# Feed-forward, attention, feed-forward of a macaron layer: three phases one after the other, or one phase in which the feed-forwards run piecewise inside the attention of a neighbouring batch

## The reference

```python
x = x + 0.5 * ffn(layernorm(x))                 # first feed-forward, gives x1
x = x + attn(layernorm(x))                      # gives x2
x = x + 0.5 * ffn(layernorm(x))                 # last feed-forward, same weights

def fp4(x):      # blocks of 16 along the last axis
    scale = max(max|block| / 6, 1e-12)
    return round |block| / scale to {0, .5, 1, 1.5, 2, 3, 4, 6}, sign back, * scale

def ffn(x):      # 128 -> 352 -> 128, every operand through fp4
    h = silu(fp4(x) @ fp4(w_gate).T) * (fp4(x) @ fp4(w_up).T)
    return fp4(h) @ fp4(w_down).T

def attn(x):     # 16 heads of 64, softmax over 512 keys
    o = softmax(q @ k.T / 8) @ v
    y = o @ w_proj + b_proj + x
    return layernorm(y, eps=1e-6) * gamma + beta
```

## Time and profile before

| | us |
|---|---|
| median of 3 runs (2581.35 to 2583.0) | 2582.26 |
| profiled execution, its own time | 2578.82 |
| span from the first to the last instruction | 2577.0 |
| mean granted clock of PE | 0.931 of 2.4 GHz |
| busy: PE, DVE, ACT, POOL | 2293.6, 1475.1, 1248.3, 1320.6 |

### The profile page before, as it was taken

The page is one execution under the profiler, slowest core; times in us unless marked ns, Lnnn a source line. Parts: engine busy times, 40 slices in busy tenths (PEclk is TensorE's granted clock), DMA queues, the critical chain, the costliest instruction groups (busy, mean ns, idle before and its releaser), DMA issues. The chain is left out here.

```text
span 2577.0 us, 39199 instructions
## 1 busy us (share of the span) xinstructions
PE 2293.6 (89%) x13353; PEld 1218.7 (47%) x13353; DVE 1475.1 (57%) x2161; ACT 1248.3 (48%) x1848; POOL 1320.6 (51%) x852
## 2 busy tenths in 40 slices
PE   3768759999999999999999999999999999566776
PEld 2545524545444444444444444444445455244444
DVE  5898844455445444544444444445445455389986
ACT  3555535455545445544544454455445455344454
POOL 3565625555545555555554555555555555355553
PEclk8887769999999999999999999999999999677778
DMA  4100000000000000000000000000000000000100
GB/s 122 33 25 25 19 21 6 2 6 7 2 7 2 6 3 6 6 2 7 2 6 3 6 2 6 7 2 6 2 7 2 6 2 2 18 17 26 31 20 21
DMA packets 182697, 32.50 MB, mean 13 GB/s; under 512 B 149184, under 2 KB 176000, under 8 KB 182528
## 3 DMA queue, kind: packets, MB, share of 16 engines
q1 hardware_dynamic: 182528, 30.17, 6.5%
HBM read 15.42 MB, written 8.39 MB: 9 GB/s over the span
## 5 line engine op out<-in xcount | busy, mean ns | idle before, releaser
L852 DVE TENSOR_REDUCE nmax<-pX 128x2 fp32r<-128x1024 f32 x512 | 626.9, 1225 | 336.6 <-PE pX L912 323.3
L795 POOL TENSOR_TENSOR ES<-ES,E 128x1024 f32<-128x1024 f32 x256 | 607.9, 2375 | 337.6 <-ACT E L807 337.5
L807 ACT ACTIVATE E<-pS 128x1024 f32<-128x1024 f32 x512 | 524.5, 1024 | 467.0 <-PE pS L901 392.6
L791 POOL TENSOR_TENSOR ES<-E 128x1024 f32<-128x1024 f32 x128 | 303.8, 2373 | 555.7 <-ACT E L807 555.7
L927 PE MATMUL pO<-E,VA 128*64 128x512 f32 x2048 | 555.5, 621 | 0.0
L885 PE MATMUL pM<-xf,w_raw 128*64 128x512 f32 x1024 | 268.6, 603 | 8.5 <-DMA xf<-xhT 6.2
L901 PE MATMUL pS<-QH,KH 64*128 64x512 f32 x1024 | 256.0, 497 | 19.4 <-issue 19.3
L901 PEld LDWEIGHTS pS<-QH,KH 64*128 64x128 f32 x1024 | 95.5, 183 | 358.6 <-ACT E L807 183.8
L865 DVE TENSOR_TENSOR ON<-OT,pM 128x512 f32<-128x512 f32 x128 | 88.0, 687 | 263.7 <-PE pM L971 263.7
L912 PE MATMUL pX<-KH,QH 64*128 64x512 f32 x1024 | 231.6, 416 | 4.0 <-DVE nmax L852 2.6
L901 PE MATMUL pS<-SH,onesr 64*128 64x512 f32 x1024 | 203.5, 394 | 0.0
(11 more groups left out here) (145 smaller groups left out, 3167.0 us busy)
## 6 DMA issues: line engine op xcount, KB each, us to landing
RROW<-RC SPq DMA_DIRECT2D x512, 2.0 KB, 2.0
Fxin<-in_L_attn_x SPq DMA_DIRECT2D x16, 256.0 KB, 2.7
Y<-in_L_attn_x SPq DMA_DIRECT2D x16, 256.0 KB, 4.8
x<-Fxout SPq DMA_DIRECT2D x16, 256.0 KB, 2.0
xf<-xhT SPq DMA_DIRECT2D x16, 256.0 KB, 2.3
SH<-nmax SPq DMA_DIRECT2D x256, 2.0 KB, 2.0
LC<-LROW SPq DMA_DIRECT2D x256, 2.0 KB, 2.0
Lx1in<-x SPq DMA_DIRECT2D x16, 256.0 KB, 2.7
```

Source lines behind the costliest of these rows:

```text
L791: g.tensor_tensor(ES[par][:, :, :], E[0][:, :, :], E[1][:, :, :], ALU.add).then_inc(s_add, 1)
L795: g.tensor_tensor(ES[par][:, :, :], ES[par][:, :, :], E[s][:, :, :], ALU.add).then_inc(s_add, 1)
L807: a.activation(E[s][:, :, :], pS[:, :, :], ACT.Exp).then_inc(s_exp, 1)
L852: v.tensor_reduce(nmax[px % 2][:, :, t:t + 1], pX[:, :, :], AX.X, ALU.max, negate=True).then_inc(s_max, 1)
```

## The change

One program without phases. In the 32 steps of attention of batch b run pieces of the first feed-forward of batch b + 1 and of the last one of batches b - 1 and b - 2. A table by step number t = 4 p + s says which piece; each engine has four such functions (`first_ffn_psum`, `last_ffn_psum` before the step's own work, `first_ffn`, `last_ffn` behind it; on PE and POOL only the last two). Steps run over b from -2 to 17, so that batch -1 has only the first feed-forward of batch 0 and batches 16 and 17 have only the ends.

- Each feed-forward has one PSUM bank, `pF`, through which turned x, gate tiles, up tiles, turned h tiles and the down product go one after the other. Silu of g is made as g (1 + tanh(g/2)) / 2: tanh on ACT, two operations on DVE.
- h is quantized in two halves (704 elements per partition each) and in place.
- All feed-forward matmuls, the turns too, are ordinary products in halves of 64 output rows.
- The projection of a pair goes into `pX[:, 0]` and DVE adds it to `Yacc` in SBUF; `pY` and the matmul that loaded it from `Y` are gone. On PE the projection now stands ahead of K.
- x1, the norm of x1 and y stay in SBUF for two batches; the DRAM tensor, `xhT` and `Y` are gone. x is loaded and the result stored by SP once a batch, in the fifth and the fourth pair.
- POOL's sums over the exponential are two operations of 512 each instead of one of 1024.
- V's tiles run three rounds ahead instead of four.

What runs at which step t (b is the batch of the attention around it; F is the first feed-forward, L the last):

| engine | F of b + 1 (norm and rounding of x: b + 2) | L of b - 2 (t to 11), of b - 1 (from t = 10) |
|---|---|---|
| PE | turn x 0, gate 1-4, up 5-8, turn h 12-15, down 16, turn x1 20 | up 0-2, turn h 6-9, down 10; turn x 26, gate 27-30, up 31 |
| ACT ahead of the exponential | copy x 1, tanh 2-5, copy h 13-16, copy x1 21 | copy h 7-10; copy x 27, tanh 28-31 |
| ACT behind | magic h 9, 11; scale x1 19; scale x 22; magic x 25 | magic h 3, 5; scale y 13; scale x2 18; magic x 22 |
| DVE ahead of the maxima | silu 2-5, h 6-9, x1 = pF + xin 17 | h 0-3, x2 + pF 11; silu 28-31 |
| DVE behind | maxima of h 7, 9; round h 10, 12; norm of x1 17, 18; norm of x 19, 21; maxima of x 23; round x 26 | maxima of h 1, 3; round h 4, 6; norm of y 10, 12; gamma and x2 14; norm of x2 15, 17; maxima of x 20; round x 24 |
| POOL ahead of its sum | divide h 8, 10; rescale h 11, 13; roots 18, 20; + bias 21, + beta 22; divide x 24; rescale x 27 | divide h 2, 4; rescale h 5, 7; roots 11, 16; divide x 21; rescale x 25 |

```diff
-        ffn_block(False)
-        attention(nc, w_raw, s_raw, w_proj, ident, xhT, Y)
-        ffn_block(True)
+    def steps(eng, body):
+
+        for b in range(-2, 2):
+            for p in range(PAIRS):
+                body(b, p, b % 2)
+        with eng.Fori(0, (B - 4) // 2) as c:
+            for bpar in (0, 1):
+                for p in range(PAIRS):
+                    body(2 * c + 2 + bpar, p, bpar)
+        for b in range(B - 2, B + 2):
+            for p in range(PAIRS):
+                body(b, p, b % 2)
...
+    def pe_gate(self, pe, c, k):
+
+        if k == 0:
+            pe.wait_ge(self.s_xqT, c + 1)
+        else:
+            pe.wait_ge(self.s_silu, 4 * c + k)
+        for n in range(2):
+            ins = self.nc.tensor.matmul(self.pF[half(n), 0:FF], self.xqT[:, k * 128 + 64 * n:k * 128 + 64 * n + 64],
+                                        self.wguT[:, 0, 0:FF], start=True, stop=True)
+        ins.then_inc(self.s_gate, 1)
...
+    def act_tanh(self, act, c, k):
+
+        act.wait_ge(self.s_gate, 4 * c + k + 1)
+        self.nc.scalar.activation(self.row(k), self.pF[:, 0:FF], ACT.Tanh, scale=0.5).then_inc(self.s_tanh, 1)
...
+    def dve_silu(self, dve, c, k):
+
+        dve.wait_ge(self.s_tanh, 4 * c + k + 1)
+        self.nc.vector.scalar_tensor_tensor(self.row(k), self.row(k), 1.0, self.pF[:, 0:FF],
+                                            ALU.add, ALU.mult).then_inc(self.s_silu, 1)
...
+                        first_ffn_psum(b, t, bpar)
+                        last_ffn_psum(b, t, bpar)
                         if s == 3 and there(i - 2, NP):
                             dve.wait_ge(s_rb, i - 1)
                             wait(dve, s_proj, i - 2)
...
+                        if s == 1 and there(i - 3, NP):
+                            bo, yp = (b, bpar) if p >= 3 else (b - 1, 1 - bpar)
+                            dve.wait_ge(s_proj, i - 2)
+                            dve.wait_ge(s_y0, bo + 1)
+                            wait(dve, s_yacc, i - 3)
+                            v.tensor_tensor(Yacc[yp][:, :], pX[:, 0, :], Yacc[yp][:, :], ALU.add).then_inc(s_yacc, 1)
...
+                        first_ffn(b, t, bpar)
+                        last_ffn(b, t, bpar)
                 steps(dve, body)
...
-                def project(b, p):
+                def project(i, p):
...
                     pe.wait_ge(s_norm, i - 2)
+                    pe.wait_ge(s_max, 4 * min(i + 2, NP) if isinstance(i, int) else 4 * (i + 2))
+                    wait(pe, s_yacc, i - 3)
                     for t in range(T):
                         for n in range(2):
-                            ins = pe_.matmul(pY[half(n), t * 128:(t + 1) * 128],
+                            ins = pe_.matmul(pX[half(n), 0, t * 128:(t + 1) * 128],
                                              ON[:, t * 128 + 64 * n:t * 128 + 64 * n + 64], wp[:, po, :],
-                                             start=False, stop=po == PAIRS - 1 and t == T - 1)
+                                             start=True, stop=True)
...
+                        first_ffn(b, 4 * p + s, bpar)
+                        last_ffn(b, 4 * p + s, bpar)
                         if s == 0 and there(i + 2, NP):
...
+                        if s == 1 and there(i - 3, NP):
+                            project(i, p)
                         if s == 1 and there(i + 2, NP):
                             pe.wait_ge(s_qlo, i + 3)
                             per_head(1, p2, x).then_inc(s_k, 1)
-                        if s == 1 and there(i - 3, NP):
-                            project(b, p)
...
+                            for hd in range(2):
+                                ins = g.tensor_tensor(ES[par][:, hd, :], ES[par][:, hd, :], E[s][:, hd, :], ALU.add)
+                            ins.then_inc(s_add, 1)
```

More of the change, by code:

```diff
@@ L149, in __init__ @@
-        self.val = [mem.sb(f"{name}_val{i}", [128, n * BLK]) for i in range(2)]
-        self.magic = [mem.sb(f"{name}_magic{i}", [128, n * BLK]) for i in range(2)]
+        self.amax, self.scale, self.tie, self.inv = (
+            mem.sb(f"{name}_{k}", [128, n]) for k in ("amax", "scale", "tie", "inv"))
         self.s_amax = mem.sem(f"{name}_s_amax")
@@ L179, in divide @@
+    def divide(self, nc, pool, c, val, b):
         pool.wait_ge(self.s_inv, c + 1)
[L180 to L187 removed]
@@ L637, in attention @@
-def attention(nc, w_raw, s_raw, w_proj, ident, xhT, Y):
-    v, a, g, pe_ = nc.vector, nc.scalar, nc.gpsimd, nc.tensor
     KT = S // 128
@@ L799, in _, with first_ffn_psum @@
             def _(act):
+                F.qh.magics(nc, act, 0, F.mag[:, 0:NW], F.h[:, 0:NW])
+                for k in range(3):
+                    act.wait_ge(s_wT_ps, k + 1)
+                    src = (pO, pM, F.pF)[k]
+                    dst = wguT[:, k, :] if k < 2 else wdT[:, :, :].rearrange("p t d -> p (t d)")
+                    a.activation(dst, src[:, 0:FP], ACT.Copy, scale=1.0 if k < 2 else 0.5).then_inc(s_wT, 1)
+                def first_ffn_psum(b, t, bpar):
+                    c = b + 1
+                    if there(c, B):
+                        if t == 1:
+                            F.act_x(act, c)
+                        if 2 <= t < 6:
+                            F.act_tanh(act, c, t - 2)
+                        if 13 <= t < 17:
+                            F.act_h(act, c, t - 13)
+                        if t == 21:
+                            act.wait_ge(s_xmT_ps, c + 1)
+                            a.activation(xf[1 - bpar][:, :], F.pF[:, :], ACT.Copy).then_inc(s_xf, 1)
@@ L817, in body @@
                             a.activation(KH[(p + 2) % 4][:, :], pM[:, :], ACT.Copy).then_inc(s_khi, 1)
-                        if s == 2 and p == 2 and (not isinstance(b, int) or b > 0):
-                            act.wait_ge(s_proj, PAIRS * b)
-                            a.activation(batch(b - 1), pY[:, :], ACT.Copy).then_inc(s_yout, 1)
                         if s == 2 and there(i - 1, NP):
```

1004 lines of the change are left out of this document (501 added, 503 removed).

## The result

The changed kernel took 2626.18 us (median of 4 runs, 2624.8 to 2628.3) against 2582.63 us before (2581.35 to 2586.6), a ratio of 1.0166 with a 95% interval of 1.0150 to 1.0182. That is 52 us over the forecast of 2574 and on the other side of "before". It is inside the wide range (2430 to 2670), which had room for the rivals, but 11 us outside the forecast's own (2535 to 2615), and among the prices of rival 3 (2606 to 2638); of the chances given, "slower" (0.43) came in. Differences under 5 us are not read here. Three single runs, one of the kernel before and two of experiment 3, took 3750 to 5600 us, and the ratios leave them out.

What follows compares the result with a forecast made beforehand. Attention was taken as bound by PE, the feed-forward phases as chains filling no engine. Start 105 + attention (1825.4 + 336 - 10 + 231) + end 81 = 2568 us span, 2574 forecast; own range 2535 to 2615, 8 in 10 2430 to 2670.

Steps and rivals of the forecast that it cites:

- rival 3: Attention: PE waits lower its clock, 2 to 4 us lost a batch, 2606 to 2638 us; chance 0.10.
- the start: Before attention's scores: batch 0's feed-forward runs alone at the low clock, first scores at 105 us.
- the waits in s1: Second step of each pair: PE's projection waits for that step's maxima, delayed by DVE tails; 9.4 us a batch.
- those of the other steps: Waits at t=2, 11, 14, 18, 24, and 4 with 20, from late DVE or ACT work; 6.3 us a batch.
- The 0.5 us of a bare s1: s1 without feed-forward work: projection ahead of K waits for the maxima, 0.5 us longer; 65 us in all.
- The rival that the tails hide: Attention: ACT and DVE run ahead, waits fall toward the 65 us floor; 2408, half way 2490; chance 0.30.
- a turned h tile, 6 such matmuls, 0.67: PE's feed-forward work: each turned h tile takes 0.67 us, four tiles in each feed-forward.
- the step t=11: Rounding and moments of y at t=10 meet POOL's sums; ON, awaited by PE's V block, comes 2.65 us late.
- rival 2: POOL and DVE share SBUF access, DVE tails wait for POOL's sums; 2644 to 2714 us; chance 0.20.
- The price of 0.89 a rounding: DVE tails: rounding half of h is two operations of 0.89 us, 1.82 with its own wait.
- Behind the last scores: End: batch 14's last feed-forward ends at about 24 us, then batch 15's runs; 81 us in all.
- Of 752 us of phases: Feed-forward phases outside attention: 566 of 752 us go, and 557 come back inside attention.

Runs made afterwards that it cites:

- experiment 3: Changed kernel with POOL's sum of the exponentials at t=10 cut to 8 columns of each half instead of 512: 2576.82 us, ratio 0.9976.
- experiment 8: Kernel before, without interleaving, with only the projection put ahead of K in s1, waiting for the maxima: 2645.4 us, ratio 1.0250.
- experiment 7: Changed kernel with K ahead of the projection on PE and DVE's sum into `Yacc` behind KL: 2550.68 us, ratio 0.9883.
- experiment 9: Changed kernel with DVE's feed-forward pieces of s0 ahead of QL: 2583.58 us, ratio 1.0007.
- experiment 10: Changed kernel with 64-wide h pieces, K ahead of the projection, s0 pieces ahead of QL, moments of y behind ON: 2420.78 us, ratio 0.9385.
- experiment 1: Changed kernel with all six pieces of a turned h tile 64 features wide, none 32: 2582.95 us, ratio 1.0007.
- experiment 4: Changed kernel with POOL's sums whole again, one operation of 1024 columns instead of two of 512: 2659.18 us, ratio 1.0304.
- experiment 5: Changed kernel with two unneeded tiles computed on PE at t=11 while it waits for ON: 2607.79 us, ratio 1.0104.

## Why the prediction came out on the wrong side

**What held.** What bounds the kernel, the start (104.0 against 105), the pieces on PE except one, the places and causes of most waits. By the steps' lengths above, less the matmuls in them, the waits in s1 come to 7.7 us a batch against 9.4 forecast (t=5: 1.96 against 2.17, t=13: 1.11 against 1.78, t=17: 1.00 against 1.14, t=21: 1.63 against 1.84, t=25: 1.73 against 1.87; by its own terms the forecast for t=5 is 2.12 and for t=13 1.75), those of the other steps to 6.7 against 6.3. That the second sum agrees is luck: t=11 has 3.66 for 2.65, t=19 and 23 have 1.1 that was not forecast, and t=18 and 24, forecast at 1.2, have none. The 0.5 us of a bare s1 measured 0.53 by itself (experiment 8). The rival that the tails hide (2408 to 2490) was wrong about the changed kernel: PE's waits are there. That they can be hidden was shown only by other orders (experiments 7, 9, 10).

**What failed: the term "a turned h tile, 6 such matmuls, 0.67".** It took 0.89 for 8 matmuls of one width and scaled by the count, although one of the six is 32 wide, a form that the trace of before does not show. It measured 1.09, eight times a batch, 43 us in all (experiment 1). By the rule of bounding what the trace does not show, it should have had two ends.

**And the step t=11.** The prediction had it late by 2.65 us and named POOL's sums there, but at the duration of an unheld tail. PE's step grew by 3.66 us (3.46 to 7.12): when one sum of POOL is away 2.15 go (experiment 3), 1.79 of lateness and 0.36 of clock. That is the mechanism of rival 2, which "decides from 0.6 us a batch on"; but the places where a hold was found on PE's path are t=11 and, with less, t=19 (experiment 4), not eight, so 2644 to 2714 was too slow. The price of 0.89 a rounding came from the first of the two roundings (1.62 us for 1408 elements); the second (line 198 of the kernel before, last feed-forward) took 2.24 on the mean in the same trace, in those looked at beside a POOL division of 1.06 us, and that was not used. The wait of 3.07 us was followed by a clock of 0.50, which the forecast put at nothing: 1.4 us a batch in t=12 and 0.36 in t=11, and 18 us less in all when PE is kept busy (experiment 5). That is rival 3 at the same place, a little under its price of 2 to 4 us a batch; that the measured time lies among its 2606 to 2638 is luck, since the clock is some 20 of the 52 us over the forecast.

**The sum of it.** Per batch against the forecast: h tiles 8 x 0.42 = +3.4, clock in t=12 +1.4, waits (with the 0.36 of clock in t=11) 14.4 against 15.7 = -1.3, so +3.5, and some 45 us over 13 full batches; the stretch measured +39. Behind the last scores, +17: the feed-forward of batch 14 ends 37 us behind them (its down product from 2558.1 to 2562.2) where the forecast had 24, and batch 15 alone takes the other 61 where it had 57. Eight h tiles run there at the low clock with 2.11 us each, where twice 0.67 is 1.34, which is 6 of the 17; PE also waits 2.7 us for one up tile and 4.1 us for the quantized h of batch 14. What is left was not taken apart. With the forecast 9 us below before, the h tiles, the clock or the tail alone would have been enough to turn its sign; undoing the first alone brings the kernel to before (1.0007).

**What the change is worth.** Of 752 us of phases 550 went (566 forecast), and 596 came back between the first and the last scores (557 forecast). 326 of these are the matmuls as summed; the other 270 are waits, dear h tiles and low clock. Most of that was a matter of order: who stands behind whom on PE in s1 (75 us, each edit alone), on DVE at t=10 (63) and in s0 (43), and of the width of one piece (43). The four together take 197 of the 270 back (in experiment 10 the stretch is 2224.7 us, 101.7 to 2326.4). With order and width mended the same change is 6% faster than before instead of 1.7% slower.

## What to carry to other kernels

Where work is woven into a full engine, price each wait it brings by what stands behind the waiting instruction, and then move that, before judging the idea: here three reorderings and the width of one piece were worth 43 to 75 us each, where 44 us was the distance to the kernel before. Put DVE operations that read only SBUF behind the one that PE waits for, and keep POOL's operations short: in the rows here a hold lasted to the end of the operation that held. Count a matmul of a width that the trace does not show as unknown, above all one that stands alone among others.
